# State sums of two of four tiles by accumulating transpositions, in a perceiver layer with a selective scan

## The chip, the cores and the metric

One core of a Trainium2 chip. The metric is the device time in microseconds of one execution, as the median of three runs. Engines: PE (matmul; PEld is its weight load), DVE (vector), ACT (scalar), POOL (GpSimd), and SP, which only issues transfers.

## What is computed

The input is 128 sequences of 32 tokens of 256 features, with 257 context rows for each sequence. All arithmetic is float32 but for the feed-forward weights and activations, which are small integers in bfloat16. Cut to what matters:

```python
x = x + cross_attention(layernorm(x), ctx)
x = x + mixer(layernorm(x))
x = x + feed_forward(layernorm(x))        # quantised weights (-1, 0, 1) and activations (8 bit)

# mixer: 512 channels, 16 states
h = x @ in_w.T + in_b
u = silu(depthwise_conv3(h) + conv_b)
x_dbl = u @ x_proj_w.T + x_proj_b         # 64 columns for delta, 16 for B
delta = softplus(x_dbl[..., :64] @ dt_w.T + dt_b)
state[l, d, n] = exp(delta[l, d] * A[d, n]) * state[l-1, d, n] + delta[l, d] * u[l, d] * B[l, n]
y[l, d] = sum_n state[l, d, n] + u[l, d] * D[d]
out = y @ out_w.T + out_b
```

The change is about the sum over n in the line before the last.

## The kernel before, in words

The 4096 tokens are worked on in 8 blocks of 512 (16 sequences). In the mixer the partitions are 128 of the 512 channels (a tile; there are 4, numbered 0 to 3) and the free dimension is the block's 512 tokens.

A tile has 16 states. They are taken in 11 slots (`SCAN`, line 149): slots 0, 2, 4, 6, 8 hold two states, slots 1, 3, 5, 7, 9, 10 hold one. Each slot goes through the engines so: ACT makes the decay with one exp for each state, from delta, into PSUM (line 641; the buffer of a slot is free when the scan two slots back is done); POOL multiplies w = delta * u with the broadcast B rows into one of 8 state buffers (line 576); DVE runs the scan in place over the state buffer (line 853); and PE adds the states up in the PSUM tensor `acc`, by a matmul of each state with the identity (line 977 is the helper `mm`, which records every plain matmul). A float32 matmul shows as two records. To spare PE work, POOL first adds the two states of slots 2, 4 and 6 of each tile into one (`PAIRED`, line 584, four slots behind its own product), and PE takes that one sum two slots later. When all states of a tile are in `acc`, DVE adds u * D (line 844, the function `y`): for tiles 0 to 2 right after scan 0 of the next tile (`Y_AT`), for tile 3 as the step `y_last`. PE may not start the next tile's sum in `acc` before that.

The order is written out by hand. The program runs in phases of 44 slots, each slot two steps (88 steps). A phase does three things at once: "pre" of block j (attention, conv, silu, x_proj, softplus: table `PRE`), the scan slots of block j-1, and "post" of block j-2 (output projection and feed-forward: table `POST`). The scan slots stand on the odd steps, shifted by `LEAD` for each engine: POOL three slots ahead of DVE, ACT one ahead, PE one behind. The tables give the step at which every engine issues its piece of a part; each engine follows its list strictly in order, and parts on one step follow the order of the tables. The first block's preparation uses `PREPARE` as well; the last block's feed-forward has no scan beside it and uses `LAST`, in which only the order on each engine counts.

Parts the text speaks of. Pre: `stats1`, `rstd1`, `xn1` (first layernorm on DVE, POOL, ACT); `turn1`, `turn2` (transposing the normalised rows on PE); `attn_out`, `x1` (output of the attention, added on DVE); `mix_in` (PE), `u_evac` (ACT), `conv` (DVE, lines 966 and 969), `silu` (ACT, line 740), `x_proj` (PE) and `x_dbl` (ACT), `b_load` (B broadcast to `brep` by DMA), `dt` (PE), `softplus` (ACT, line 764), `times_u` (POOL, line 607). Post: `out_proj`, `x2` (DVE, line 874), `stats3`, `xn3`, `x_max` (DVE, line 882), `x_turn`, `x_evac`; and then eight halves (two to a group of 128 tokens) of `up` (PE, gate and up products), `tanh` (ACT, line 668), `gate` (DVE, line 902), `hidden` (DVE, line 911), and four groups of `h_max` (DVE, line 915), `scale_h` (ACT, line 672), `h_turn` (PE, line 1095, eight 128x128 transpositions), `h_evac` (ACT, line 678), `down` (PE), `finish` (DVE, line 927).

ACT has to load a table when it goes from exp to silu or softplus and when it comes back (rows ACT_TABLE_LOAD).

## Time and profile before

| | |
|---|---|
| median of 3 runs | 1105.43 us (1104.5 to 1112.4) |
| the profiled execution | 1107.78 us, of which the span of the profile is 1106.0 us |
| mean granted PE clock | 0.942 of full speed |
| busy over the span | PE 943.5, DVE 903.5, POOL 857.9, ACT 755.4 us |
| one full phase, 439.1 to 559.5 | 120.4 us |

The profile comes from one execution, so durations and the span belong together; the median is of other executions. PE's matmuls are pipelined and their ends are modelled: the time that a run of matmuls takes of PE is read from the starts, from its own first to the next work's.

### The profile page before, as it was taken

The numbers are of one execution on the slowest core, as the hardware profiler recorded it, in microseconds if no ns is written. First come the engines' busy times: TensorE is split into PE (matmuls) and PEld (weight loads), VectorE is DVE, ScalarE is ACT, GpSimd is POOL, SyncE is SP. The second block draws the span as 40 slices with busy tenths as digits, with TensorE's granted clock in tenths as the row PEclk, the third lists the DMA queues.
The fourth block names the chain that finished last, engine by engine and source line by source line (L and its number), as shares of the span: only waits on it lengthen the run. The fifth ranks groups of instructions, "written<-read, shape, count | busy, mean of one in ns | idle before, by whom it ended". The sixth has DMA issues, their size and how long they took to land.

```text
span 1106.0 us, 12743 instructions
## 1 busy us (share of the span) xinstructions
PE 943.5 (85%) x4007; PEld 491.5 (44%) x4042; DVE 903.5 (82%) x1210; ACT 755.4 (68%) x1320; POOL 857.9 (78%) x617
## 2 busy tenths in 40 slices
PE   6765698899989998999999998999899999777755
PEld 4441344354545453544545454545355454432333
DVE  2312687889998999899998999899989998799935
ACT  1216566787598769877798759876887768655524
POOL 0532999797979988897979797988879797989700
PEclk9778799999999999999999999999999999889967
DMA  9633252414205440525233420544042302200000
GB/s 342 218 131 123 107 178 91 164 60 165 109 21 191 159 166 20 192 77 177 91 120 118 169 111 20 191 153 172 20 172 96 115 20 82 110 0 1 27 12 20
DMA packets 22059, 124.71 MB, mean 113 GB/s; under 512 B 3496, under 2 KB 4136, under 8 KB 9449
## 3 DMA queue, kind: packets, MB, share of 16 engines
q1 hardware_dynamic: 16376, 89.09, 22.1%
q10 hardware_dynamic: 5616, 34.81, 8.2%
q8 instruction: 33, 0.54, 0.2%
q14 instruction: 34, 0.27, 0.1%
HBM read 115.23 MB, written 8.65 MB: 112 GB/s over the span
## 4 chain that ended last, share of the span: by engine, by line
PE 32%; ACT 22%; DVE 21%; POOL 10%; issue 9%; DMA 3%; SPq 1%; ACTq 0%; DVEq 0%; POOLq 0%
PE bank L977 19%; DVE state L853 10%; PE acc L977 10%; ACT decay L641 6%; POOL state L576 5%; DVE sg L902 2%; POOL rstd L539 2%; DVE hid L911 2%; DMA brep<-b_scratch 2%; POOL w L607 2%; ACT u L732 2%; ACT soft L627 2%; DVE hm L915 2%; ACT L740 2%; PE bank L1095 2%
## 5 line engine op out<-in xcount | busy, mean ns | idle before, releaser
L853 DVE TENSOR_TENSOR_SCAN state<-decay,state 128x512 f32<-128x512 f32 (+1 forms) x352 | 589.7, 1696 | 64.7 <-ACT decay L641 48.2
L576 POOL TENSOR_TENSOR state<-w,brep 128x512 f32<-128x512 f32 (+1 forms) x352 | 612.4, 1765 | 24.2 <-PE acc L977 24.0
L977 PE MATMUL acc<-state,ident 128*128 128x512 f32 x832 | 406.6, 608 | 12.9 <-DVE state L853 8.8
L641 ACT ACTIVATE decay<-delta,neg_a 128x496 f32<-128x496 f32 x512 | 327.3, 669 | 75.6 <-DVE state L853 68.9
L977 PEld LDWEIGHTS acc<-state,ident 128*128 128x128 f32 x832 | 148.0, 193 | 166.2 <-issue 110.3
L584 POOL TENSOR_TENSOR state<-state 128x512 f32<-128x512 f32 x96 | 122.2, 1273 | 61.5 <-DVE state L853 61.5
L668 ACT ACTIVATE sg<-bank,ag 128x512 f32<-128x512 f32 x64 | 43.6, 682 | 62.1 <-PE bank L977 61.4
L977 PE MATMUL bank<-xn_t,in_w 128*128 128x512 f32 x128 | 63.6, 632 | 7.6 <-DVE u L969 5.6
L607 POOL TENSOR_TENSOR w<-delta,u 128x512 f32<-128x512 f32 x32 | 39.9, 1266 | 36.2 <-ACT delta L764 36.2
L977 PE MATMUL bank<-out_w,u 128*128 128x256 f32 x256 | 57.4, 382 | 6.7 <-DVE u L844 6.7
L977 PE MATMUL bank<-u,xp_w 128*81 128x512 f32 x64 | 41.1, 803 | 19.2 <-ACT u L740 19.2
L977 PEld LDWEIGHTS bank<-out_w,u 128*128 128x128 f32 x256 | 48.0, 190 | 19.6 <-DVE u L844 13.4
L627 ACT ACTIVATE soft<-x_in,nmr,rstd 128x256 f32<-128x256 f32 x64 | 33.2, 589 | 33.7 <-POOL nmr L542 33.3
L902 DVE SCALAR_TENSOR_TENSOR sg<-sg,bank 128x512 f32<-128x512 f32 x64 | 43.0, 671 | 16.1 <-ACT sg L668 16.1
L678 ACT ACTIVATE hq_t<-bank,unmagic 128x512 bf16<-128x512 f32 x64 | 40.5, 679 | 16.9 <-PE bank L1095 16.8
L1095 PE MATMUL bank<-ident,hid 128*128 128x128 f32 x256 | 37.7, 289 | 12.6 <-ACT hid L672 10.4
L1120 PE MATMUL bank<-ident,soft 128*128 128x128 f32 x128 | 20.6, 312 | 31.7 <-ACT soft L627 31.7
L1095 PEld LDWEIGHTS bank<-ident,hid 128*128 128x128 f32 x256 | 31.0, 148 | 31.9 <-ACT hid L672 16.6
L911 DVE TENSOR_TENSOR hid<-sg,bank 128x512 f32<-128x512 f32 x64 | 42.7, 668 | 0.6 <-PE bank L977 0.2
L977 PE MATMUL bank<-up_q,xq_t 128*128 128x512 bf16 x128 | 40.5, 400 | 3.1 <-DVE hid L911 3.0
L977 PEld LDWEIGHTS bank<-xn_t,in_w 128*128 128x128 f32 x128 | 23.8, 200 | 43.3 <-issue 35.4
L977 PE MATMUL bank<-gate_q,xq_t 128*128 128x512 bf16 x93 | 32.4, 401 | 10.9 <-DVE sg L902 2.8
(137 smaller groups left out, 1306.8 us busy)
## 6 DMA issues: line engine op xcount, KB each, us to landing
keys<-in_keys_t SPq DMA_DIRECT2D x32, 1028.0 KB, 4.8
keys<-in_keys_n SPq DMA_DIRECT2D x32, 1024.0 KB
brep<-b_scratch ACTq DMA_DIRECT2D x32, 1024.0 KB, 6.8
x_scratch<-x_in SPq DMA_DIRECT2D x8, 512.0 KB, 2.6
res<-x_scratch SPq DMA_DIRECT2D x8, 512.0 KB, 3.2
out<-res SPq DMA_DIRECT2D x8, 512.0 KB, 8.6
x_in<-in_x SPq DMA_DIRECT2D x7, 512.0 KB, 5.4
brep<-in_w_gateT SPq DMA_DIRECT2D x1, 1024.0 KB, 13.4
```

The costliest lines, as they stand in the source:

```text
L576: nc.gpsimd.tensor_tensor(state[state_buffer(odd, g)][:, 0:count, :], w[:, m, :].unsqueeze(1).to_broadcast((P, count, TOK)), brep[:, n:n + ...
L584: nc.gpsimd.tensor_tensor(s[:, 0, :], s[:, 0, :], s[:, 1, :], ALU.add).then_inc(paired, 1)
L607: nc.gpsimd.tensor_tensor(w[:, g, :], delta[:, g, :], u[par][:, g, :], ALU.mult)\
L627: nc.scalar.activation(to[:, i, :], x[:, i, :], ACT.Identity, bias=nmr[k][:, i:i + 1], scale=rstd[k][:, i:i + 1]).then_inc(xn_ready[k], 1)
L641: last = nc.scalar.activation(decay[:, to + i, :, 1:LEN], d, ACT.Exp, scale=neg_a[:, m, n + i:n + i + 1])
L668: nc.scalar.activation(sg[g % 2][:, :], bank[:, ffn_banks(g // 2, scan)[0], :], ACT.Tanh, scale=ag[:, g // 2:g // 2 + 1]).then_inc(gate_ta ...
L678: nc.scalar.activation(hq_t[:, k * KT // 2:(k + 1) * KT // 2, :].rearrange("p k t -> p (k t)"), bank[:, ffn_banks(g, scan)[k], :], ACT.Ide ...
L853: nc.vector.tensor_tensor_scan(flat, decay[:, of:of + count, :, :].rearrange("p c q l -> p (c q l)"), flat, 0.0, ALU.mult, ALU.add).then_i ...
L902: nc.vector.scalar_tensor_tensor(sg[g % 2][:, :], sg[g % 2][:, :], 1.0, bank[:, up_a, :], ALU.add, ALU.mult).then_inc(gated, 1)
L911: nc.vector.tensor_tensor(hid[g // 2 % 2][:, half], sg[g % 2][:, :], bank[:, up_b, :], ALU.mult)\
L977: return nc.tensor.matmul(o, l, r, start=first, stop=last)
L1095: last = nc.tensor.transpose(bank[:, to[2 * k // KT], k % (KT // 2) * P:(k % (KT // 2) + 1) * P], hid[g % 2][:, k * P:(k + 1) * P], ident[ ...
```

## The change

Tiles 1 and 2 (`TURNED`) are summed in another way. POOL adds no pairs for them. For each of their 16 states PE issues four 128x128 matmuls with `is_transpose`, the state's 128 tokens as the stationary operand and the identity as the moving one, accumulating in the four quarters of `acc`. So `acc` holds the sum transposed. ACT copies it to a new SBUF tensor `y_t` (behind its exps of slot 2 of the next tile), PE transposes it back into `acc` (in its slot 1 of the next tile, which is DVE's slot 2), and DVE's y comes after scan 2 of the next tile rather than after scan 0. PE's sums of slots 0 to 2 of tiles 2 and 3 are put off to its slot 2. Tiles 0 and 3 are summed as they were, pairs included. All five tables of steps are written anew; of these the diff below shows the entries that the text speaks of.

```diff
--- before.py
+++ after.py
@@ -35,102 +35,102 @@
...
-    ("tanh", [14, 17, 21, 26, 37, 45, 52, 68]),
+    ("tanh", [14, 16, 19, 23, 40, 45, 54, 68]),
-    ("up", [12, 13, 21, 25, 36, 46, 51, 65]),
+    ("up", [12, 13, 17, 22, 40, 47, 51, 67]),
-    ("h_turn", [29, 35, 68, 78]),
+    ("h_turn", [27, 36, 71, 77]),
-    ("h_evac", [32, 36, 71, 77]),
+    ("h_evac", [28, 37, 70, 80]),
...
 PRE = [
-    ("stats1", [1]),
+    ("stats1", [0]),
-    ("xn1", [4]),
+    ("xn1", [6]),
-    ("mix_in", [58, 58, 60, 61]),
+    ("mix_in", [52, 52, 59, 64]),
-    ("silu", [62, 67, 67, 68]),
+    ("silu", [59, 69, 70, 70]),
-    ("x_proj", [67]),
+    ("x_proj", [72]),
-    ("x_dbl", [72]),
+    ("x_dbl", [73]),
-    ("softplus", [81, 87]),
+    ("softplus", [81, 85]),
-    ("times_u", [82, 82, 87, 87]),
+    ("times_u", [81, 82, 83, 85]),
...
 LAST = [
-    ("up", [21, 21, 27, 28, 41, 51, 78, 81]),
+    ("up", [33, 39, 47, 55, 71, 72, 85, 87]),
-    ("tanh", [17, 25, 25, 25, 44, 59, 71, 79]),
+    ("tanh", [25, 31, 47, 56, 58, 78, 86, 86]),
-    ("gate", [16, 27, 32, 38, 70, 72, 78, 79]),
+    ("gate", [25, 38, 42, 66, 72, 80, 84, 85]),
-    ("hidden", [16, 27, 37, 40, 71, 72, 78, 80]),
+    ("hidden", [31, 38, 54, 67, 79, 80, 84, 86]),
-    ("h_max", [33, 52, 76, 86]),
+    ("h_max", [53, 68, 81, 86]),
-    ("scale_h", [26, 29, 77, 81]),
+    ("scale_h", [47, 61, 83, 87]),
-    ("h_turn", [38, 42, 86, 87]),
+    ("h_turn", [61, 74, 84, 87]),
-    ("h_evac", [28, 58, 79, 87]),
+    ("h_evac", [53, 78, 84, 87]),
-    ("down", [40, 73, 86, 87]),
+    ("down", [61, 78, 86, 87]),
-    ("finish", [68, 73, 87, 87]),
+    ("finish", [62, 83, 87, 87]),
...
 PREPARE = [
-    ("total", [12]),
+    ("total", [26]),
-    ("scales", [23]),
+    ("scales", [26]),
-    ("quantise", [44, 50, 52, 59]),
+    ("quantise", [7, 34, 64, 70]),
...
@@ -154,21 +154,34 @@
 
 
 
-PAIRED = (2, 4, 6)
+
+TURNED = (1, 2)
+PAIRED = [m * CPT + c for m in range(TILES) if m not in TURNED for c in (2, 4, 6)]
 PAIR_LAG = 4
-SUMS = [[k for k in range(CPT) if k + 2 * (k in PAIRED) == c] for c in range(CPT)]
-SUM_SLOTS = [c for c in range(CPT) if SUMS[c]]
-
-
-def sums_to(g):
-
-    m, c = divmod(g, CPT)
-    return m * len(SUM_SLOTS) + SUM_SLOTS.index(c + 2 * (c in PAIRED)) + 1
-
-
-def pairs_to(g):
-    m, c = divmod(g, CPT)
-    return m * len(PAIRED) + PAIRED.index(c) + 1
+
+COPY_AT, TURN_AT, READ_AT, SUM_AT = 2, 1, 2, 2
+
+
+def _sums():
+    plan = [[] for _ in range(SLOTS)]
+    for s in range(SLOTS):
+        m, c = divmod(s, CPT)
+        c += 2 * (s in PAIRED)
+        plan[m * CPT + (max(c, SUM_AT) if m - 1 in TURNED else c)].append(s)
+    return plan
+
+
+SUMS = _sums()
+SUM_ORDER = [s for step in SUMS for s in step]
+
+
+def sums_to(s):
+
+    return SUM_ORDER.index(s) + 1
+
+
+def pairs_to(s):
+    return PAIRED.index(s) + 1
 
 
 def slots_to(n):
@@ -270,6 +283,7 @@
         p_t = sb("p_t", [P, 2, P])
         pl_t = sb("pl_t", [P, P])
         z = sb("z", [P, DIM])
+        y_t = sb("y_t", [P, TOK])
         x_dbl = sb("x_dbl", [XROWS, TOK])
 
         xq_t = sb("xq_t", [P, HALVES, TOK], bf16)
@@ -386,8 +400,10 @@
         decay_ready = sem("decay_ready", SLOTS)
         input_ready = sem("input_ready", SLOTS)
         scan_done = sem("scan_done", SLOTS)
-        paired = sem("paired", TILES * len(PAIRED))
-        summed = sem("summed", TILES * len(SUM_SLOTS))
+        paired = sem("paired", len(PAIRED))
+        summed = sem("summed", SLOTS)
+        sums_copied = sem("sums_copied", len(TURNED))
+        sums_turned = sem("sums_turned", len(TURNED))
         y_ready = sem("y_ready", TILES)
 
         mixed = sem("mixed", 2)
@@ -578,7 +594,7 @@
                             w[:, m, :].unsqueeze(1).to_broadcast((P, count, TOK)),
                             brep[:, n:n + count, :], ALU.mult).then_inc(input_ready, 1)
                         done = g - PAIR_LAG
-                        if done >= 0 and done % CPT in PAIRED:
+                        if done in PAIRED:
                             reach(pool, scan_done, b, done + 1)
                             s = state[state_buffer(odd, done)]
                             nc.gpsimd.tensor_tensor(s[:, 0, :], s[:, 0, :], s[:, 1, :], ALU.add).then_inc(paired, 1)
@@ -641,6 +657,10 @@
                             last = nc.scalar.activation(decay[:, to + i, :, 1:LEN], d, ACT.Exp,
                                                         scale=neg_a[:, m, n + i:n + i + 1])
                         last.then_inc(decay_ready, 1)
+                        if m - 1 in TURNED and g % CPT == COPY_AT:
+                            reach(act, summed, b, m * CPT)
+                            reach(act, sums_turned, b, TURNED.index(m - 1))
+                            nc.scalar.activation(y_t[:, :], acc[:, :], ACT.Copy).then_inc(sums_copied, 1)
                     elif part == "mixer_weights":
                         act.wait_ge(w_loaded, 16 * 8)
                         nc.scalar.activation(neg_a[:, :, :], neg_a[:, :, :], ACT.Exp).then_inc(prep_a, 1)
@@ -840,7 +860,10 @@
                         nc.vector.bn_aggr(mv[k][:, i, :], raw[k][:, i, :]).then_inc(moments_ready[k], 1)
 
                 def y(block_, odd, m):
-                    reach(dve, summed, block_, (m + 1) * len(SUM_SLOTS))
+                    if m in TURNED:
+                        reach(dve, sums_turned, block_, TURNED.index(m) + 1)
+                    else:
+                        reach(dve, summed, block_, (m + 1) * CPT)
                     nc.vector.scalar_tensor_tensor(u[odd][:, m, :], u[odd][:, m, :], cols[:, D_SKIP, m:m + 1],
                                                    acc[:, :], ALU.mult, ALU.add).then_inc(y_ready, 1)
 
@@ -852,7 +875,7 @@
                         flat = state[state_buffer(odd, g)][:, 0:count, :].rearrange("p c t -> p (c t)")
                         nc.vector.tensor_tensor_scan(flat, decay[:, of:of + count, :, :].rearrange("p c q l -> p (c q l)"),
                                                      flat, 0.0, ALU.mult, ALU.add).then_inc(scan_done, 1)
-                        if g % CPT == Y_AT and m:
+                        if m and g % CPT == (READ_AT if m - 1 in TURNED else Y_AT):
                             y(b, odd, m - 1)
                     elif part == "qk":
                         qk()
@@ -1003,22 +1026,38 @@
                     after(pe, hid_ready, b, halves)
                     after(pe, hq_t_ready, b, 2 * turned)
 
+                def turn_sums(block_, m):
+                    reach(pe, sums_copied, block_, TURNED.index(m) + 1)
+                    for q in range(GROUPS):
+                        last = nc.tensor.transpose(acc[:, q * P:(q + 1) * P], y_t[:, q * P:(q + 1) * P], ident[:, :])
+                    last.then_inc(sums_turned, 1)
+
                 for part, b, g, odd in slots("tensor", j, par, pre, scan, post):
                     if part == "chunk":
                         m, c = divmod(g, CPT)
-                        if c == 0:
-
-                            reach(pe, y_ready, b, m)
-                        for k in SUMS[c]:
-                            s = m * CPT + k
-                            if k in PAIRED:
+                        if c == TURN_AT and m - 1 in TURNED:
+                            turn_sums(b, m - 1)
+                        for s in SUMS[g]:
+                            n, count = SCAN[s][1:3]
+                            if n == 0:
+
+                                reach(pe, y_ready, b, m)
+                            if s in PAIRED:
                                 reach(pe, paired, b, pairs_to(s))
                             else:
                                 reach(pe, scan_done, b, s + 1)
-                            for i in range(1 if k in PAIRED else SCAN[s][2]):
-                                last = mm(acc[:, :], ident[:, :], state[state_buffer(odd, s)][:, i, :],
-                                          k == 0 and i == 0, k == CPT - 1)
-                        if SUMS[c]:
+                            for i in range(1 if s in PAIRED else count):
+                                one = state[state_buffer(odd, s)][:, i, :]
+                                if m in TURNED:
+
+                                    for q in range(GROUPS):
+                                        part_t = slice(q * P, (q + 1) * P)
+                                        last = nc.tensor.matmul(acc[:, part_t], one[:, part_t], ident[:, :],
+                                                                start=n + i + q == 0,
+                                                                stop=n + i == STATES - 1 and q == GROUPS - 1,
+                                                                is_transpose=True)
+                                else:
+                                    last = mm(acc[:, :], ident[:, :], one, n + i == 0, n + count == STATES)
                             last.then_inc(summed, 1)
                     elif part == "vo":
                         pe.wait_ge(v_loaded, 16 * 4)
```

## Rows read from the trace of the kernel before

**Rows 1.** The page, part 1: busy time, share of the span, instructions.

```profile
PE 943.5 (85%) x4007; PEld 491.5 (44%) x4042; DVE 903.5 (82%) x1210; ACT 755.4 (68%) x1320; POOL 857.9 (78%) x617
```

**Rows 2.** One phase: us; busy PE, PEld, DVE, ACT, POOL; clock, DMA, GB/s.

```profile
439.10:559.50 120.40, 111.53 (x496) 58.24 (x500) 111.05 (x149) 94.03 (x166) 104.89 (x75) 0.99 0.34 123
```

**Rows 3.** Waits of DVE, 318 to 920: us in total, times, longest.

```profile
DVE state L853 <- ACT decay L641: 22.3, 34, 1.7
DVE u L844 <- PE acc L977: 6.1, 5, 1.2
```

**Rows 4.** Waits of ACT and of POOL, 318 to 920.

```profile
ACT sg L668 <- PE bank L977: 38.4, 21, 4.4
...
POOL state L584 <- DVE state L853: 46.0, 25, 2.9
```

**Rows 5.** PE in order of time: start, us, what, count, idle before.

```profile
438.80 5.36 PE L977 MATMUL bank<-u,xp_w 128*81 128x512 f32 x8 [2.19 <-ACT u L740]
443.99 1.04 PE L1095 MATMUL bank<-ident,hid 128*128 128x128 f32 x8
444.86 2.74 PE L977 MATMUL acc<-state,ident 128*128 128x512 f32 x6
447.44 1.04 PE L977 MATMUL bank<-down_q,hq_t 128*128 128x256 bf16 x8
...
559.21 3.66 PE L977 MATMUL bank<-u,xp_w 128*81 128x512 f32 x8 [2.19 <-ACT u L740]
```

**Rows 6.** Groups by form, whole span: busy us, mean ns, idle before.

```profile
L977 PE MATMUL acc<-state,ident 128*128 128x512 f32 x832 | 406.6, 608 | 12.9 <-DVE state L853 8.8 <-DVE u L844 4.1
L641 ACT ACTIVATE decay<-delta,neg_a 128x496 f32<-128x496 f32 x512 | 327.3, 669 | 75.6 <-DVE state L853 68.9 <-issue 5.8
L977 PEld LDWEIGHTS acc<-state,ident 128*128 128x128 f32 x832 | 148.0, 193 | 166.2 <-issue 110.3 <-DVE state L853 42.6 <-DVE u L844 5.7
L584 POOL TENSOR_TENSOR state<-state 128x512 f32<-128x512 f32 x96 | 122.2, 1273 | 61.5 <-DVE state L853 61.5
...
L689 ACT ACTIVATE xn_t<-bank 128x512 f32<-128x512 f32 x32 | 17.6, 588 | 5.1 <-PE bank L1120 5.1
```

**Rows 7.** DVE in order of time, one phase's waits: start, us, idle before.

```profile
441.36 3.41 DVE L853 TENSOR_TENSOR_SCAN state<-decay,state 128x1024 f32<-128x1024 f32 x2 [0.46 <-ACT decay L641]
...
447.71 2.29 DVE L853 TENSOR_TENSOR_SCAN state<-decay,state 128x1024 f32<-128x1024 f32 x1 [1.22 <-ACT decay L641]
...
459.42 2.34 DVE L853 TENSOR_TENSOR_SCAN state<-decay,state 128x512 f32<-128x512 f32 x2 [1.72 <-ACT decay L641]
462.98 0.75 DVE L844 SCALAR_TENSOR_TENSOR u<-u,cols,acc 128x512 f32<-128x512 f32 x1 [1.22 <-PE acc L977]
...
523.07 2.29 DVE L853 TENSOR_TENSOR_SCAN state<-decay,state 128x1024 f32<-128x1024 f32 x1 [0.66 <-ACT decay L641]
...
532.71 0.69 DVE L960 TENSOR_TENSOR x_in<-bank,x_in 128x512 f32<-128x512 f32 x1 [0.41 <-PE bank L977]
```

**Rows 8.** DVE in order of time, the first scans.

```profile
108.90 2.29 DVE L853 TENSOR_TENSOR_SCAN state<-decay,state 128x1024 f32<-128x1024 f32 x1 [16.17 <-POOL state L576]
...
127.67 3.48 DVE L853 TENSOR_TENSOR_SCAN state<-decay,state 128x512 f32<-128x512 f32 x2 [3.03 <-ACT decay L641]
```

**Rows 9.** DVE in order of time, the last feed-forward.

```profile
1083.39 0.48 DVE L927 SCALAR_TENSOR_TENSOR res<-bank,beta,res 128x256 f32<-128x256 f32 x1 [0.33 <-PE bank L977]
1085.30 0.69 DVE L902 SCALAR_TENSOR_TENSOR sg<-sg,bank 128x512 f32<-128x512 f32 x1 [1.42 <-ACT sg L668]
...
1090.87 0.68 DVE L902 SCALAR_TENSOR_TENSOR sg<-sg,bank 128x512 f32<-128x512 f32 x1
...
1094.84 1.22 DVE L915 TENSOR_REDUCE hm<-hid 128x1 f32<-128x1024 f32 x1
...
1102.44 0.48 DVE L927 SCALAR_TENSOR_TENSOR res<-bank,beta,res 128x256 f32<-128x256 f32 x1 [5.10 <-PE bank L977]
```

**Rows 10.** Granted PE clock where x_proj runs: start:end us, busy, clock.

```profile
439.00:441.50 2.50, 2.50 (x4) 0.54 0.00 0
```

118 lines of the change are left out of this document (59 added, 59 removed).

## The prediction, made blind

> **What bounds the kernel now.** I read the busy times first: over the whole run PE is busy 85%, DVE 82%, POOL 78% and ACT 68% of the span [rows 1]. No engine is full on average, but the run has a start and an end in which only part of the work exists, so the next view is the one by stretches. One full phase (44 slots; scan of one block, attention of the next, feed-forward of the one before) takes 120.40 us from 439.1 to 559.5. In it DVE is busy 111.05 us, PE 111.53, POOL 104.89 and ACT 94.03, with a granted PE clock of 0.99 [rows 2]. So DVE and PE are level at 92%. They differ in kind: DVE is in order and its scans are the recurrence that everything else feeds; PE runs ahead or behind within eight state buffers.
>
> What keeps DVE from 111 us is its own waits. In the five full phases (318 to 920) the longest is that of the scan for ACT's decay, 22.3 us in 34 times, or 4.5 us a phase; then y for PE's sums, 6.1 us, once a phase [rows 3]. The scan waits on POOL in no row there: POOL's pair adds wait for DVE instead, 46.0 us, and ACT's tanh waits for PE 38.4 us [rows 4]. POOL therefore has slack, and PE acts on DVE only by way of ACT: a late PE holds tanh, an evacuation or x_dbl, the next exp comes late, and a scan waits. DVE's 9.35 us of idle time in the phase is then the most that a change which leaves DVE's own work alone can win there.
>
> **The change, part by part.** All durations are those of the profiled execution (1107.78 us, span 1106.0), which is 2.35 us above the median of 1105.43.
>
> *PE, sums of tiles 1 and 2.* A plain state sum is two records of a 128x512 matmul against ident; six start at 444.86 and what follows starts at 447.44, so 0.43 us each and 0.86 us a state [rows 5]. With the pairs folded a tile has 13 such sums: 11.2 us. The new form is four 128x128 transpositions a state. Eight transpositions of the same kind start at 443.99 and the next work at 444.86: 0.109 us each, their weight loads hidden [rows 5]. A tile has 16 states, 64 transpositions, 7.0 us, and 0.44 us to turn the sum back. PE so loses 3.8 us a tile, 7.5 us a phase, 60 us in 16 tiles. From both sides: if every transposition in this place cost the whole mean load time of the acc loads, it would be 64 x 0.193 [rows 6] = 12.4 us a tile, 1.6 us more than now with the turn; I take 0.109, the row of the same instruction. None of the 7.5 us is path by itself, because PE is not what DVE waits for, except through ACT.
>
> *POOL, pair adds.* 96 adds of 1273 ns become 48 [rows 6]: 61 us less busy, 7.6 us a phase, and half of their waits. The scans wait for nothing of POOL's, so the direct gain is nothing.
>
> *ACT, one copy for each turned tile.* A PSUM copy of 128x512 takes 588 ns [rows 6], 9.4 us in 16. ACT is idle 26 us a phase [rows 2]; cost nothing if the copy does not wait. What is queued behind it is the exp of slot 3 and all that follows, and the scan waits for that.
>
> *The chain scan, sum, copy, turn, y.* Let T be the end of a turned tile's last scan. The copy stands behind the exp of slot 2 of the next tile, which needs scan 0 (a double scan, 2.29 us [rows 7]) and takes 2 x 0.67 us [rows 6]: T+3.6. The copy ends at T+4.2, four transpositions and the handing over at about T+5. DVE comes to y after scans 0, 1 and 2: T+2.3+1.2+2.3 = T+5.8 at the least. So y is covered by 0.8 us, if PE reaches the last sum and the turn in time. Behind PE's wait stand the deferred sums of slots 0 to 2, the attention work, and ACT for the results of that. Bounds: from -0.1 us a place (the few waits of y at tiles 1 and 2 go) to +1.2 us, the longest wait of y now [rows 3]; over 16 places -2 to +19 us. I take 0, the chain's own count. The eight-buffer ring covers the deferral: POOL is three slots ahead and needs slot 0's buffer again at its slot 8.
>
> *The new plan of steps.* Every table is rewritten, so each wait in the phase may move. Some stay by construction. One is 1.72 us before the scan at 459.42: after a double scan, ACT must do a table load, two softplus, a load and the exp before it. Softplus stays at step 81 and scan 42 behind it. Another is y_last for PE, 1.22 us at 462.98 [rows 7]: tile 3 is summed as before. The second softplus moves from step 87 to 85, ahead of the exp of the next block's slot 0, and stats1 from step 1 to 0, ahead of its scan. That is an exchange: about 3.8 us of ACT now lies before that exp, and 1.9 us of stats lie over it. The waits that PE's queue makes may go. At 447.71 the scan waits 1.22 us; ACT was behind because h_turn of group 2 was queued behind x_proj. In the new plan h_turn (71) is ahead of x_proj (72), but x_dbl follows at 73 rather than 72 and may wait itself. With 0.46 us at 441.36, 0.66 at 523.07 and 0.41 at 532.71 [rows 7], and two of 0.17 and 0.27 us like them, 3.2 us a phase are within reach of a lighter PE. Bounds 0 and -3.2; I take half, -1.6, because the late silu, x_proj and softplus chain is still one chain. Over seven phases with scans (the first and the last are like the five in this): -11.2 us.
>
> *Start.* In the first block softplus of both pairs now runs before the first exp. That saves ACT two table loads, but the first scan (108.90) may come up to 1.6 us later. After it, scans wait for decay 3.03 us at 127.67 [rows 8] and about as much twice before. stats1 and xn1 are also moved. Bounds +1.6 and -5; I take -2. The quantise steps (now 7, 34, 64, 70) come in POOL's order still before the first brep load, and the scales two attention groups later, with nobody waiting: 0.
>
> *End.* The last feed-forward is serial, so its order is its time. Before, tanh and gate of half 3 ran before finish of group 0 (1083.39), half 4 started gate at 1085.30, half 6 at 1090.87, the last h_max at 1094.84 and the last finish at 1102.44 [rows 9]. In the new LAST table finish 0 (62) stands before gate 3 (66), so gate 3, hidden 3 and h_max 1 (0.7+0.7+1.8 us) come after 1083.9 and gate 4 starts at about 1087.1, 1.8 us later. tanh 6 (86) stands behind h_evac 2 (84), which needs h_max 2, scale_h 2 and h_turn 2: gate 6 at 1096.1 rather than 1090.9. up 7 stands behind down 2. The last h_max starts at about 1099.4, 4.6 us later, and 7.6 us from there to the last finish stay. Bounds +3 and +6; I take +4.6.
>
> **Sum.** -11.2 (phases) - 2.0 (start) + 4.6 (end) = -8.6: 1107.8 - 8.6 = 1099.2 as profiled, and 2.35 less as a median, 1096.8. Forecast 1097 us, 0.8% faster. About 1% is what a measurement of this kernel can tell from no change.
>
> **Rivals.** *A, the slack reaches DVE in full.* All of the 3.2 us a phase go, and the replan saves another 1.2 of the waits I held fixed: 7 x 4.4 = 31 us; with -3 and +4.6, 1107.8 - 29 = 1079 profiled, 1076. With the 3.2 alone it is 1084. For it: PE and POOL both get 7.5 us of room. Against: the largest of the waits (1.72 us) stands at a table load that stays.
>
> *B, the PE clock falls where state sums are gone; this one ends slower.* From 439.0 to 441.5 the granted clock is 0.54, the lower of the two levels (1.2 and 2.4 GHz) for nearly all of it [rows 10], after PE had waited 2.19 us for u. The eight x_proj matmuls then took 5.36 us; in the next phase, after the same 2.19 us but with the clock kept, 3.66 [rows 5]. That is 1.7 us of PE and it ended in the 1.22 us DVE wait. Today the sum matmuls fill such gaps. In the second half of tile 2 (steps 53 to 67) the other PE work is little more than mix_in, so transpositions and idle time would be alone there. With two more such falls a phase, each passed on as 1.22 us of DVE, 2.44 x 7 = +17 us, and the 1.6 us gain a phase is not made: 1107.8 + 17 - 2 + 4.6 = 1127 profiled, 1125. One such fall more a phase gives 1116. It decides from 1.3 more falls a phase, where they eat the gain. Against: in 559.2 to 562.9 the clock survived a thin stretch.
> The Trainium skill, "TensorE: Matmul & The Clock Gate", Part 4 (PE-mode transpose), speaks for it: transposing does not count as PE-busy in the same way and does not bring the full clock. No row here has a long run of transpositions alone, so the trace cannot say; by that rule the sum would be rival B's.
>
> *C, the new waits bind.* y, copy and turn miss their 0.8 us of cover by the upper bound in half of the places: +9.6 us, which with the forecast's other terms is 1106: no change. It needs PE's queue to be over 0.8 us late at the turn.
>
> **How the numbers follow.** Forecast 0.50 (1087 to 1105, so 0.20 of it faster by over 1%, 0.30 same). A 0.20, all faster. B 0.18, of it 0.16 slower. C 0.12, of it 0.05 same and 0.07 slower (where every place misses). That makes faster 0.40, same 0.37, slower 0.23. The range 1077 to 1119 leaves out the far end of A and the worse half of B.
>
> **What would show it.** Right: a phase near 118.8 us with DVE still busy 111; PE busy near 104 and POOL near 97 in it; 1024 transpositions in acc for state sums plus 64 turning back, at 0.109 us each when queued; y of tiles 1 and 2 with under 0.3 us of wait; the last gate-to-finish stretch 4 to 5 us longer. Wrong: granted clock under 0.97 in the stretches of tile 2; scans waiting on ACT for over 6 us a phase; y or the copy among the largest waits; or a phase near 116, which would be A.

## The result, and the profile after

The kernel after the change takes 1119.68 us (median of 10 runs) against 1104.80 us for the kernel before on the same chip: ratio 1.0135, 95% interval 1.0105 to 1.0166. The change makes it 1.3% slower; the forecast was 0.8% faster. The profiled execution took 1120.12 us with a span of 1118.3, against 1107.78 and 1106.0 before: 12.3 us to explain (the medians are 14.9 apart).

The page of the kernel after, part 1 (answers to [rows 1]):

```profile
PE 914.5 (82%) x4714; PEld 550.3 (49%) x4714; DVE 902.9 (81%) x1210; ACT 764.5 (68%) x1334; POOL 798.7 (71%) x569
```

PE is 29 us less busy, POOL 59 us less, ACT 9 us more, and DVE unchanged to 0.6 us: the work moved as forecast. The time is therefore DVE's idle time. Phases are read best from y_last to y_last (L844 before, L867 after, the last of a block's four). Before, these starts are 120.25, 120.27, 119.10, 120.21, 121.72, 120.25 and 105.33 us apart; after, 119.87, 122.92, 122.71, 122.96, 119.46, 122.82 and 107.68. The first of them comes at 216.88 rather than 222.46 (start: -5.6), the last finish 59.50 us after the last of them rather than 52.85 (end: +6.65). The seven phases hold the rest, +11.3. (Each is read from one execution; how far the start scatters is said in its place.)

Two phases of the kernel after, a long and a short one (columns as in [rows 2]):

```profile
459.67:582.38 122.71, 107.66 (x584) 65.85 (x584) 110.93 (x148) 95.41 (x168) 97.48 (x69) 0.96 0.33 121
705.34:824.80 119.46, 106.51 (x584) 65.17 (x584) 110.81 (x149) 95.44 (x168) 97.68 (x69) 0.97 0.33 120
```

DVE's work is the same 110.9 us in both, and in [rows 2]. So a full phase of this kernel has two lengths, 119.5 to 119.9 and 122.7 to 123.0, and neither is the forecast's 118.8. The question is what makes it long. Waits of DVE over the five phases from 318 to 920 (as in [rows 3]), then of POOL (as in [rows 4]):

```profile
DVE state L876 <- ACT decay L657: 19.0, 16, 3.0
DVE res L897 <- DMA res<-x_scratch: 7.6, 3, 2.9
DVE u L867 <- PE acc L1000: 6.8, 5, 1.4
```

```profile
POOL ve L552 <- DVE mv L860: 64.3, 10, 9.8
POOL state L592 <- PE acc L1055: 25.8, 10, 3.3
```

The scans wait less for decay in total than in [rows 3] (19.0 for 22.3) and half as often, but the longest is 3.0 us rather than 1.7; a row is new, x2 waiting for the DMA that brings res. y has the same five waits as before, all for tile 3 (releaser L1000): none for a turned tile. POOL waits a lot and nobody for it.

Where x2 waits, in DVE's order of time, early in two of the long phases; the short phase from 705.34 has no such row:

```profile
467.71 0.69 DVE L897 TENSOR_TENSOR res<-bank,res 128x512 f32<-128x512 f32 x1 [2.28 <-PE bank L1000]
...
590.02 0.69 DVE L897 TENSOR_TENSOR res<-bank,res 128x512 f32<-128x512 f32 x1 [1.87 <-DMA res<-x_scratch]
```

The first is put down to PE, whose bank had long been there; the load issued at 460.51 lands 7.1 us later, when the wait ends. With it there are five in the run, 13.0 us, one in each long phase and one in the last. The issues of transfers before the first of the two, of the kernel after and then of the kernel before:

```profile
453.37 0.33 ACTq L774 DMA_DIRECT2D brep<-b_scratch  x1
454.05 0.34 SPq L528 DMA_DIRECT2D out<-res  x1
458.01 0.33 ACTq L774 DMA_DIRECT2D brep<-b_scratch  x1
458.59 0.33 ACTq L774 DMA_DIRECT2D brep<-b_scratch  x1
460.51 0.32 SPq L506 DMA_DIRECT2D res<-x_scratch  x1
```

```profile
455.48 0.33 ACTq L754 DMA_DIRECT2D brep<-b_scratch  x1
456.38 0.33 ACTq L754 DMA_DIRECT2D brep<-b_scratch  x1
457.73 0.34 SPq L512 DMA_DIRECT2D out<-res  x1
466.28 0.32 SPq L490 DMA_DIRECT2D res<-x_scratch  x1
```

The phase itself ends at 459.67 in the first and at 462.98 in the second. Counted from there, the new plan issues the last two brep loads (1 MB each) 5.8 and 5.5 us later and the res load 2.5 us earlier, one on the other. The res load goes in both kernels as soon as the out store ahead of it has landed; that took 6.4 us here and 8.5 before, where it was the store that stood beside the brep loads. The page's part on DMA issues, after (3.2 us to landing before):

```profile
res<-x_scratch SPq DMA_DIRECT2D x8, 512.0 KB, 6.9
```

Why has the phase from 705.34 no such wait? Its issues:

```profile
698.76 0.34 SPq L528 DMA_DIRECT2D out<-res  x1
699.23 0.33 ACTq L774 DMA_DIRECT2D brep<-b_scratch  x1
701.73 0.32 SPq L506 DMA_DIRECT2D res<-x_scratch  x1
```

The x_proj before it was slow (below), so the second brep load comes behind the out store and not 0.7 us ahead of it; the store lands in 2.9 us, and the res load goes 3.6 us ahead of y_last. In this plan a slow x_proj at the end of one phase spares the next one its wait for res; so it does twice more in the kernel with `LAST` put back.

The second kind of wait is at the end of a phase. The end of the phase 582 to 705, DVE in order of time; in the others one row of 1.91 us stands in place of the first two:

```profile
696.07 2.29 DVE L876 TENSOR_TENSOR_SCAN state<-decay,state 128x1024 f32<-128x1024 f32 x1 [1.07 <-ACT decay L657]
701.78 2.34 DVE L876 TENSOR_TENSOR_SCAN state<-decay,state 128x512 f32<-128x512 f32 x2 [3.04 <-ACT decay L657]
705.34 0.75 DVE L867 SCALAR_TENSOR_TENSOR u<-u,cols,acc 128x512 f32<-128x512 f32 x1 [1.22 <-PE acc L1000]
```

PE in that place, then in the short phase after it:

```profile
679.00 0.95 PE L1032 MATMUL acc<-ident,y_t 128*128 128x128 f32 x4 [2.48 <-ACT y_t L663]
679.74 1.92 PE L1134 MATMUL bank<-ident,hid 128*128 128x128 f32 x8
682.66 1.86 PE L1000 MATMUL bank<-down_q,hq_t 128*128 128x256 bf16 x8 [1.00 <-ACT hq_t L698]
...
800.27 0.66 PE L1032 MATMUL acc<-ident,y_t 128*128 128x128 f32 x4 [2.63 <-ACT y_t L663]
800.77 1.04 PE L1134 MATMUL bank<-ident,hid 128*128 128x128 f32 x8
803.57 1.03 PE L1000 MATMUL bank<-down_q,hq_t 128*128 128x256 bf16 x8 [1.76 <-ACT hq_t L698]
```

PE now stands 2.5 us for the copy of the turned sum before it comes to h_turn, down and x_proj. In the first case the clock then falls: eight transpositions take 1.92 us and not 1.04, the down 1.86 and not 1.03. In the second, after the same stop, it holds. Of the six x_proj in full phases this one alone is slow here (4.46 us, the others 3.63). In the kernel before five of six were slow; the sixth, the fast one of [rows 5] at 559.21, ends the one phase of 119.10 us.

The end, DVE (answers to [rows 9]):

```profile
1107.14 1.22 DVE L938 TENSOR_REDUCE hm<-hid 128x1 f32<-128x1024 f32 x1
...
1114.80 0.48 DVE L950 SCALAR_TENSOR_TENSOR res<-bank,beta,res 128x256 f32<-128x256 f32 x1 [5.43 <-PE bank L1000]
```

### The profile page after: what moved, and what is told of

Its sections match the earlier page's. It is cut to its first block, busy times and chain, and to the rows that moved or that the text cites. A ratio compares the mean times of both kernels' runs of the same rounds, so it can differ in the third digit from the quotient of the medians.

```text
span 1118.3 us, 14102 instructions
## 1 busy us (share of the span) xinstructions
PE 914.5 (82%) x4714; PEld 550.3 (49%) x4714; DVE 902.9 (81%) x1210; ACT 764.5 (68%) x1334; POOL 798.7 (71%) x569
## 4 chain that ended last, share of the span: by engine, by line
PE 30%; DVE 27%; ACT 17%; issue 11%; DMA 8%; POOL 6%; SPq 1%; DVEq 0%; ACTq 0%; POOLq 0%
PE bank L1000 18%; DVE state L876 14%; ACT decay L657 5%; PE acc L1000 4%; POOL state L592 4%; DMA res<-x_scratch 3%; DMA out<-res 3%; PE acc L1055 3%; DVE sg L925 2%; DVE raw L856 2%; PE bank L1134 2%; ACT soft L643 2%; DVE hm L938 2%; ACT u L752 1%; DMA brep<-in_w_gateT 1%
## 5 line engine op out<-in xcount | busy, mean ns | idle before, releaser
L1000 PE MATMUL acc<-state,ident 128*128 128x512 f32 x416 | 203.6, 611 | 11.0 <-DVE state L876 10.9
L1055 PE MATMUL acc<-ident,state 128*128 128x128 f32 x1024 | 137.2, 281 | 12.9 <-DVE state L876 8.9
L1055 PEld LDWEIGHTS acc<-ident,state 128*128 128x128 f32 x1024 | 118.9, 145 | 38.2 <-DVE state L876 18.2
L1000 PEld LDWEIGHTS acc<-state,ident 128*128 128x128 f32 x416 | 77.7, 195 | 91.4 <-issue 62.7
L552 POOL TENSOR_TENSOR ve<-mv,eps 128x4 f32<-128x4 f32 x24 | 4.8, 202 | 118.5 <-DVE mv L860 118.5
L1000 PE MATMUL bank<-xn_t,in_w 128*128 128x512 f32 x128 | 74.5, 725 | 7.1 <-ACT xn_t L709 6.0
L600 POOL TENSOR_TENSOR state<-state 128x512 f32<-128x512 f32 x48 | 61.0, 1270 | 21.7 <-DVE state L876 21.7
L1000 PE MATMUL bank<-out_w,u 128*128 128x256 f32 x256 | 57.4, 382 | 6.7 <-DVE u L867 6.7
L1000 PEld LDWEIGHTS bank<-out_w,u 128*128 128x128 f32 x256 | 48.0, 190 | 19.6 <-DVE u L867 13.4
L1000 PE MATMUL bank<-down_q,hq_t 128*128 128x256 bf16 x256 | 37.4, 295 | 14.4 <-ACT hq_t L698 14.2
L692 ACT ACTIVATE hid<-hid,magic,sh 128x1024 f32<-128x1024 f32 x32 | 39.5, 1234 | 12.3 <-DVE sh L944 12.0
L1000 PEld LDWEIGHTS bank<-xn_t,in_w 128*128 128x128 f32 x128 | 28.3, 238 | 39.6 <-issue 30.6
```

The costliest lines, as they stand in the source:

```text
L600: nc.gpsimd.tensor_tensor(s[:, 0, :], s[:, 0, :], s[:, 1, :], ALU.add).then_inc(paired, 1)
L1000: return nc.tensor.matmul(o, l, r, start=first, stop=last)
L1055: last = nc.tensor.matmul(acc[:, part_t], one[:, part_t], ident[:, :], start=n + i + q == 0, stop=n + i == STATES - 1 and q == GROUPS - 1, ...
```

## The experiments

All ratios are to the kernel before, run on the same chip, with their 95% intervals. Theory: the loss is in the plan (the late res, the last feed-forward) and in the clock at x_proj, not in the turned sums.

**Parts of the plan put back, one at a time.** x2 alone:

```diff
-    ("x2", [3, 5]),
+    ("x2", [5, 5]),
```

> The changed kernel with one entry undone: x2 at steps 5, 5 as before instead of 3, 5. Transfer theory (five of the seven phases with scans are about 122.8 us, instead of 119.7 in the two others, because DVE stands at x2 on step 3 for 1.9 to 3.2 us until the res load has landed behind the brep loads): scan 2 now goes ahead of x2 and covers 2.3 us of that, so the waits for the load are under 1 us, the phases near 120.4, and the time 8 to 12 us under the changed kernel's 1119.7, so 1108 to 1112. Clock theory (the phases are long because the PE clock falls twice in each, at h_turn/x_turn and in the second half of tile 2): nothing moves, 1117 to 1123.

Measured 1116.61 us, ratio 1.0115 (1.0081 to 1.0149): above the 1108 to 1112 of the transfer theory, and not clear of the 1.0135 of the kernel after. Yet no x2 waits for a DMA any more in a full phase. Three of its six full phases are still long, 122.5 to 122.6, and just these have a slow x_proj (4.7 us; the others 3.6).

b_load alone, the issue of the brep loads:

```diff
-    ("b_load", [78, 84, 86, 87]),
+    ("b_load", [78, 78, 81, 84]),
```

> The changed kernel with one entry undone: b_load at steps 78, 78, 81, 84 as before instead of 78, 84, 86, 87. Transfer theory, in its sharper form (it is the four 1 MB brep loads issued late that slow the out store and the res load from about 3 us to 7): out and res land early, x2 on step 3 waits for nothing, every phase is near 119.7, the time 1105 to 1109. If x2 is simply too early whatever the loads do, the wait stays and the time is 1116 to 1122. Clock theory: 1117 to 1123.

Measured 1110.09 us, 1.0053 (1.0014 to 1.0091): one wait for res of over a microsecond is left, 1.45 us, and the medians to landing are 3.3 us for res and 8.5 for out, as before the change. Four of the six full phases are short, 119.4 to 119.9; of the two long ones one has a slow x_proj (4.67 us), the other a 2.5 us wait of DVE for tanh instead. This one line holds more than half of the loss.

The order of the last feed-forward alone (table `LAST` of before):

> The changed kernel with the table LAST as before (order of the last feed-forward). Order theory: from y_last to the last finish 59.5 us fall back to 52.9, the time falls by 6.7 us to about 1113; phases unchanged. If the end is long for the clock or the state before it and not for its order, it falls by under 2 us.

Measured 1115.13 us, 1.0083 (1.0049 to 1.0117). The end is 52.8 us from the last y, as before, for 59.5: the order of LAST costs 6.7 us in the profile (5.7 by the ratios, whose intervals overlap a little).

Both of the last two together, the base of what follows ("the mended kernel"):

> The changed kernel with two entries of the plan undone: b_load at 78, 78, 81, 84 and the table LAST as before. The two losses are in different stretches, so they should add: 9.6 us (b_load alone) and 4.6 (LAST alone) under 1119.7, so 1105.5, between 1102 and 1109; the rest over the best phase (two or three of seven phases at 122.6 for a clock fall at x_proj) stays.

Measured 1106.37 us, 1.0016 (0.9979 to 1.0053): no difference from before can be measured. This is the turned sums together with the rest of the new plan, and it is a balance: in the profiled execution the first y_last comes at 215.27 for 222.46, and the seven phases take 834.4 us for 827.1, four of the six full ones with a slow x_proj (4.75 to 4.84 us).

**Plan and sums apart.** The new sums with the tables of before, then the kernel before with the tables of after (there are four, `POST`, `PRE`, `LAST` and `PREPARE`, not the five that the section on the change speaks of):

> The turned sums of tiles 1 and 2 alone: all four tables POST, PRE, LAST, PREPARE as before the change. Plan theory (transposed sums themselves are worth a little, the new tables lose it): phases 118.5 to 120.5, no wait of x2 for the res load, start and end as before the change, 1098 to 1106. Clock theory: the clock falls twice a phase here too, phases 121 to 123, 1112 to 1122. Rival: the new copy and turn were placed for the new plan and bind in the old one: y of tiles 1 and 2 or the copy wait over 1 us each, 1108 to 1125.

> The kernel before (plain sums, pair adds on all tiles) with the four tables POST, PRE, LAST and PREPARE of the changed kernel. If the plan alone loses the time: x2 waits for the res load, the last feed-forward is 59.5 us long, 1112 to 1122. If the plan and the turned sums only belong together (plan good for a PE that is 7 us lighter): PE is behind, scans wait more for ACT, over 1120. If the loss is the turned sums' (clock falls, waits for the copy): 1100 to 1110, because the start is 5.6 us shorter and the end 6.7 longer, with one clock fall a phase.

Measured 1145.98 us, 1.0358 (1.0302 to 1.0413), and 1199.51 us, 1.0840 (1.0771 to 1.0908). Waits of DVE in the first of them:

```profile
DVE u L867 <- PE acc L1032: 40.7, 15, 3.6
```

The first is slower than any of its expectations. With the old plan y of the turned tiles waits for the turn, 2.7 us each; with the new one never. So it is the new plan that gives the turn its cover. Each half alone is far worse than both together.

**What holds the clock.** To the kernel before are added, after the last out_proj, 72 transpositions of ident into a free bank; in the second kernel instead 9 plain float32 matmuls of 512 columns (18 records):

```diff
+for i in range(72):
+    nc.tensor.transpose(bank[:, E, i % 4 * P:(i % 4 + 1) * P], ident[:, :], ident[:, :])
```

> A probe of the clock in the kernel before: after the last out_proj, where PE otherwise waits about 8 us with the clock falling from 1.00 to 0.50, it does 72 more float32 transpositions of ident into an idle bank (7.8 us at 0.109 each; extra work whose result is not used). If transpositions hold the clock like matmuls: granted clock 1.00 until they end, each 0.109 us apart, x_turn and the first up at the full rate too, and the end 1 to 3 us shorter. If they do not: the clock falls to 0.50 within them as it does now, the later ones come 0.21 to 0.22 us apart and x_turn is up to 5 us late.

> The same probe with 9 plain float32 matmuls of 128x512 (18 records, 7.7 us at 0.43 each; extra work whose result is not used) in place of the 72 transpositions. Both theories: granted clock 1.00 until they end, x_turn at 0.109 us a transposition, end 1 to 3 us shorter than in the kernel before.

PE of the first, and its stretches (clock next to last but two); then a stretch of the kernel before at the same place in its work, and one of the second kernel:

```profile
1054.45 8.02 PE L1052 MATMUL bank<-ident 128*128 128x128 f32 x72
```

```profile
1054.00:1064.00 10.00, 8.47 (x75) 8.12 (x73) 4.81 (x18) 3.25 (x7) 1.52 (x4) 1.00 0.01 2
1064.00:1074.00 10.00, 4.81 (x22) 1.90 (x22) 4.83 (x9) 4.92 (x8) 0.00 (x0) 1.00 0.00 0
```

```profile
1067.00:1077.00 10.00, 7.05 (x19) 3.00 (x20) 3.05 (x5) 4.29 (x7) 0.00 (x0) 0.50 0.00 0
```

```profile
1060.00:1068.00 8.00, 3.95 (x14) 2.08 (x14) 1.95 (x10) 4.13 (x7) 0.00 (x0) 0.63 0.00 0
```

Transpositions hold the clock: 1.00 through them and for 10 us behind, where the kernel before has 0.50. The matmuls held it no longer than the transpositions did. The 10 us behind are not sure: four more profiles below have the same 72 transpositions (this kernel again, and three others). All four show 1.00 through them, but in two of the others the clock fell 4 us behind their end. The stretch from the last y to the last finish is 50.0 us with the first and 51.0 with the second, for 52.85 (one execution each, 1101.97 and 1100.68 us). The first kernel timed:

> The kernel before with the 72 transpositions after its last out_proj, timed: the one look gave 1101.97 us with 50.0 us after the last y, against 52.85. Theory: the held clock gives back 2 to 3 us, 1101.5 to 1102.8 against 1104.5, ratio 0.9975. Rival (the look's gain was the scatter of single runs): 1104 to 1105.

Measured 1104.17 us for 1106.41, 0.9975 (0.9947 to 1.0003). It has the lowest ratio of those timed, and its gain is at the limit of what these runs can tell: the interval reaches 1. The end is 50.0 us again.

**Is the lighter PE to blame for the clock?** The mended kernel with `is_transpose=False` in the turned sums, so that the same 64 instructions a tile run as float32 matmuls (two records each, twice PE's time):

> The changed kernel with b_load and LAST undone and the sums of tiles 1 and 2 as plain float32 matmuls of the same operands (state quarter stationary, ident moving, the same transposed result) in place of is_transpose: twice the PE time, 0.215 us each, so 7 us more a phase, PE busy near 114. Clock theory (a lighter PE is why the clock falls): the falls at mix_in and x_proj go, granted clock 0.98 to 0.99 in the phases as in the kernel before; whether the time falls depends on how much of the 7 us PE hides: 1100 to 1112. Rival (the clock is incidental, the turned form has its price by its waits): the clock stays near 0.96, and with PE slower the time is over 1112.

Measured 1173.27 us, 1.0590 (1.0559 to 1.0620), over 1112 as the rival had it. PE is busy 120.6 us a phase, not 114, every full phase takes 129.5 to 129.9 us, and their granted clock is 0.96, no better than in the kernel after. But x_proj is slow in one of the six full phases alone (4.87 us, the others 3.63), for four of six in the mended kernel, and PE stops for 2.0 us at the turn, not 2.5. Both the load of PE and its stop changed, so this run does not say which of them the clock at x_proj hangs on.

**The place of copy and turn.** In the mended kernel, the copy one slot earlier; then copy, turn, read and sums all one slot earlier; then this with the 72 transpositions at the end:

```diff
-COPY_AT, TURN_AT, READ_AT, SUM_AT = 2, 1, 2, 2
+COPY_AT, TURN_AT, READ_AT, SUM_AT = 1, 1, 2, 2
```

> The changed kernel with b_load and LAST undone (1106.4 so far, phases of 119.9 or 122.4) and the copy of the transposed sum one slot earlier on ACT (COPY_AT 1 instead of 2). Theory of the stalled PE: PE stands 2.5 us at the turn of tile 2 for the copy, which ACT has behind its exps of slot 2, and the clock falls on that idle time, into x_proj, in every second phase or so, 2.7 us each; with the copy a slot (1.3 to 2 us of ACT) earlier the wait is under 1.5 us, the fall at x_proj goes in most phases, which are then 119 to 120, and the time is 1096 to 1102. Rival (the fall there comes of PE having too little work, whatever it waits for): the wait at the turn shrinks but phases of 122.4 stay as frequent, 1104 to 1108.

Measured 1118.88 us, 1.0099 (1.0065 to 1.0132). The theory missed: PE no longer stops at the turn, but 2.29 us before h_turn and 1.90 before down instead, the clock falls at x_proj in every phase, and the six full ones are all long, 122.4 to 122.9. The stop only moved.

> As e9_copy_early, and turn, deferred sums and y one slot earlier too (COPY, TURN, READ, SUM at 1, 0, 1, 1). Stalled-PE theory: the copy is ready 0.7 us after PE comes to the turn, y is 3.5 us behind the last scan and still covered, POOL waits less for state buffers (45.7 us now); 1094 to 1102, at best below e9. If one slot is too little cover: y waits over 1 us for the turn in 14 places, as in the run with the old plan, 1108 to 1125.

> As e10_turn_early with the 72 filling transpositions after the last out_proj. From the single run of the probe (y_last to last finish 50.0 us instead of 52.9) 2.9 us less than e10; by the mean of both expectations 1092 to 1099, which would be below the kernel before by 0.6 to 1.1%.

Measured 1151.29 us, 1.0377 (1.0348 to 1.0407), and 1155.56, 1.0414 (1.0378 to 1.0449). With y one slot earlier PE waits up to 4.7 us for DVE's y before it may begin tile 3, and phases are 127 to 129 us: the cover that the chain has in the code as changed is not to be shortened.

**Is it the clock, or x_proj's end?** These four start from the mended kernel. Fourteen transpositions ahead of the third down, where PE waits 1.8 us:

> The version with b_load and the last block's plan put back (1106.4 us, phases of 119.9 and of 122.5), and beside it 14 transpositions of ident ahead of the third down, in the 1.8 us in which TensorE waits for hq_t there. Theory (the clock that falls at x_proj makes the long phase, and the fall is started by the idle 2.5 us before the turn of y_t, 3 us earlier): the fill comes too late to hold the clock, so long phases stay, 1104 to 1108. Rival 1 (the wait before down starts the fall): x_proj takes 3.6 us in every phase, all phases 119.8 to 120, total 1096 to 1098. Rival 2 (the fill delays down and x_proj): every phase 0.5 to 1 us longer, 1110 to 1114.

Measured 1107.89 us, 1.0012 (0.9982 to 1.0042). The time is the theory's, and long phases stay (122.5, 122.1 and 122.0; the others 119.8 to 120.5), though x_proj takes 3.6 us in every one, as rival 1 had it. So the trace separates the two causes. (The phase of 122.5 has no fall ahead of x_proj, but a wait of 1.64 us for res.) PE in a phase of 122.06 us:

```profile
558.42 1.81 PE L1134 MATMUL bank<-ident,hid 128*128 128x128 f32 x8
560.02 2.63 PE L1143 MATMUL bank<-ident 128*128 128x128 f32 x14
562.49 1.04 PE L1000 MATMUL bank<-down_q,hq_t 128*128 128x256 bf16 x8
563.37 3.60 PE L1000 MATMUL bank<-u,xp_w 128*81 128x512 f32 x8
```

Here the clock fell and came back before x_proj (0.50 from 558.6 to 561.9, 1.00 from 562.0), which ran at full speed, but started 5.44 us after the turn, and the scan then waited 3.04 us. Where the fill took 1.69 us, x_proj started 4.2 us after the turn and the scan waited 1.91 us. So the slow clock does its harm by making x_proj end late, wherever it falls ahead of that end.

The fourth mix_in behind the up projection, to fill the stop before the turn; and the same with both fills:

```diff
-    ("mix_in", [52, 52, 59, 64]),
+    ("mix_in", [52, 52, 59, 67]),
```

> The same version with one due time changed, the fourth mix_in from slot 64 to 67: by the order of the program its 4 matmul records (1.9 us) then stand between the up projection and the turn of y_t, where TensorE now idles 2.5 to 2.6 us. Theory (that idle time starts the fall of the clock at x_proj, and the fall makes a phase of 122.5 us out of one of 119.9): the idle stretch shrinks to 0.8 us, x_proj takes 3.6 us at a granted clock of 1.00 in nearly every phase, the waits for the third tile's y and the conv after it stay away, phases 119.8 to 120.2, total 1096 to 1099. Rival (the long phase has another cause, and the slow x_proj only goes along with it): clock held, phases still 122.5, total 1105 to 1108. Second rival (the fourth conv now waits for its matmul): 0.5 to 1 us more a phase, 1110 and over.

> The late mix_in, the 14 transpositions ahead of the third down, and 72 transpositions of ident after the last out_proj, as in the fill of the kernel before. By the theory the phases are 119.8 to 120 (twice 2.5 us less than those of the late mix_in if a fall is left there) and the end after the last y is 50.0 us and not 52.8: 1093 to 1096. If neither fill adds anything to the late mix_in: 1096 to 1099. If the fills get in the way: over 1100.

Measured 1135.27 us, 1.0241 (1.0203 to 1.0280), and 1118.64 us, 1.0110 (1.0069 to 1.0150). The move missed: ScalarE's evacuation waits for the late mix_in, 2.62 us, and the copy of y_t stands behind it, so PE stopped 3.6 us before the turn instead of 2.6. The pair tells something all the same. PE without and with the fill ahead of down, the same place of a phase:

```profile
566.90 1.11 PE L1032 MATMUL acc<-ident,y_t 128*128 128x128 f32 x4 [3.61 <-ACT y_t L663]
...
570.70 1.86 PE L1000 MATMUL bank<-down_q,hq_t 128*128 128x256 bf16 x8 [0.98 <-ACT hq_t L698]
572.36 5.62 PE L1000 MATMUL bank<-u,xp_w 128*81 128x512 f32 x8
```

```profile
563.13 0.66 PE L1032 MATMUL acc<-ident,y_t 128*128 128x128 f32 x4 [3.61 <-ACT y_t L663]
...
567.69 1.04 PE L1000 MATMUL bank<-down_q,hq_t 128*128 128x256 bf16 x8
568.56 3.60 PE L1000 MATMUL bank<-u,xp_w 128*81 128x512 f32 x8
```

Same plan, same stop of 3.61 us; with the fill x_proj takes 3.60 us and not 5.62. With the fill every x_proj of a full phase takes 3.60 us. The three full phases in the middle of the run go from 126.3 to 122.9 us, 3.4 us each (the first full phase only from 124.8 to 124.0). Without the fill one x_proj of six kept the clock by itself (3.63 us), and its phase was 123.5. That is the price, in this plan, of a fall of the clock that lasts into x_proj, shown by one edit and once more inside one run (the end fill lies outside these phases). The filled kernel still has the stop and a shorter fall, and its scans wait 3.04 us in every phase.

Last, x_proj ahead of the third down, with the end fill:

```diff
-    ("h_evac", [28, 37, 70, 80]),
+    ("h_evac", [28, 37, 71, 80]),
-    ("down", [28, 61, 72, 81]),
+    ("down", [28, 61, 73, 81]),
```

> The version with b_load and the last block's plan put back (1106.4 us), with ScalarE's copies of hq_t of the third half one slot later, behind its three silus, and the third down one slot later, behind x_proj; also the 72 transpositions after the last out_proj. x_proj then waits for the last silu alone and starts about 1.2 us earlier where the clock is held and 2.0 us earlier where it falls. Theory (what makes a phase long is that x_proj ends late, by the fall of the clock or by anything else, since ScalarE's copy to x_dbl, the hidden half and delta queue up behind it): in every phase the last wait of the scans for decay is 1.9 us or less, never 3.0, also where the clock falls at x_proj; phases 119.4 to 120.3; with the end at 50.0 to 51.5 the total is 1093 to 1099, ratio 0.990 to 0.995. Rival (the slow clock costs elsewhere too, or hq_t and down, moved back, bind instead: finish of the third half or the scans' decays wait for them): phases of 121 to 123 remain, total 1102 to 1110.

Measured 1112.47 us, 1.0058 (1.0031 to 1.0085): the rival in its phases, over its range in time. PE in two phases:

```profile
437.15 5.36 PE L1000 MATMUL bank<-u,xp_w 128*81 128x512 f32 x8 [2.48 <-ACT u L760]
...
559.91 3.66 PE L1000 MATMUL bank<-u,xp_w 128*81 128x512 f32 x8 [2.48 <-ACT u L760]
```

x_proj starts 4.0 us after the turn, against 4.2 to 4.3 where the clock held and 5.0 where it fell in the mended kernel. The silu before it waits 0.92 us for DVE's last conv, so copies of hq_t moved out of its way gave little, and PE, which now stands 2.48 us before x_proj, found the clock low there in five of six full phases. The last wait for decay is 2.58 us in every phase, so the theory's 1.9 was missed too. The phases of these two are 122.7 and 121.1 us: a slow x_proj costs 1.7 us here, and it does so by the third down, now behind it: the finish waits 1.67 us in the first phase and not at all in the second.

The end was 50.0 us again, as in the kernel before with this fill. It was not in the other two kernels that have it: with the late mix_in it came out at 53.0 us (54.9 without the fills), and with the turn one slot earlier at 53.0 for 52.1, which is no gain at all.

## Why the prediction was wrong

**The step that failed is "the new plan of steps": -11.2 us for the seven phases, measured +11.3.** The prediction took the waits of before, asked which of them a lighter PE could shorten, and counted half. Those went in part: over the seven phases the scans wait for decay 23.8 us for 29.8, and x_in no longer waits for PE (2.5 before). Others grew in their place, that of the conv for ACT's u above all; after, then before, from the first y_last to the last, columns as in [rows 3]:

```profile
DVE u L989 <- ACT u L756: 7.1, 6, 1.4
```

```profile
DVE u L966 <- ACT u L736: 2.1, 6, 0.3
```

The gate's wait for tanh went from 5.6 to 7.2 us, and res was waited for 13.0 us, before 0.5. Take the 12.5 us away and the phases are about 1 us shorter than before, not 11.2 (an estimate: it takes each wait to be passed on in full). Like against like nothing was won: a phase in which neither new wait occurs is 119.5 to 119.9 us, and the one phase of before with a fast x_proj 119.1 (its scans wait 3.5 us for decay, in the phase ahead of it 4.7). The 120.4 us phase that the forecast started from had one slow x_proj in it. What the step did not do is walk the queues past each edited line. Two things that it never priced made new waits:

- `b_load` later and `x2` earlier. The res load now starts 1.9 and 2.5 us behind the last two brep loads and takes 6.9 us to land for 3.2. Five times it came late, 13.0 us together, enough for the 11.3 by which the phases grew. With x2 put back the waits are gone, with b_load put back 3.6 us of them are left, in five small ones; b_load alone brought the ratio from 1.0135 to 1.0053. Both lines are in the tables that the change rewrites, though not in the part of the diff shown above.
- The stop at the turn. The prediction asked whether y would wait for PE (it did not, in any phase), and not what PE does while ACT brings the copy: it stands for 2.5 us at tile 2's turn, shortly ahead of x_proj, and waits again for hq_t. The clock fell there in one full phase of six in the profile of after, in three with x2 put back, in one with b_load put back, and in four in the mended kernel. ACT then waits for x_dbl, for h_turn's bank and for a second dt, and the scans find their decay 1.07 and 3.04 us late instead of 1.91. The new plan also put x_proj nearer to those who need it: its start is 20 to 21 us ahead of y_last, before it was 23 to 24. So a fall costs about 2.6 us of a phase now (mended kernel: 122.5 for 119.9 in the mean); before it cost 1.1 (119.1 against 120.2), and came in nearly every phase. With x2 put back the waits for res went and two more slow x_proj came; that is why it brought so little.

**Rival B named a real cost, but not the one that made this kernel slow.** It said that the clock falls where state sums are gone, that each fall is passed on as 1.22 us, and that the time is 1116 for one more fall a phase and 1125 for two. 1119.7 lies between, and that is chance. The clock did fall more, 0.92 for 0.942 in the mean. One of the new falls stands where B put it, in the second half of tile 2, in every full phase: at mix_in (granted clock 0.50 from 660 to 665 us, for one), and the conv behind it waits 0.8 to 1.4 us for ACT's u, 0.35 before. But at x_proj the clock was low in one full phase of six, before in five, and the 11.3 us are the waits for res. Only with these mended is a fall at x_proj what makes a phase long, and then it costs 2.6 us, twice B's price. Whether the falls come of PE's lighter load, as B said, or of its stops was not separated: the fuller PE of the matmul form had its x_proj slow in one phase of six and also stopped for less time.

**The rule of the Trainium skill did not hold here.** The Trainium skill says in "TensorE: Matmul & The Clock Gate", Part 4 (PE-mode transpose), that transposing does not count as PE being busy in the same way and that the full clock does not engage for it. Here the 72 float32 transpositions in a row kept it at 1.00. They also brought it back: in the kernel with 14 of them ahead of down it was 0.50 from 558.6 to 561.9, PE did nothing but transpositions in that time, and from 562.0 it was 1.00.

**What held.** PE's loss of work: 1024 transpositions in 137.2 us of busy time, though 107 us a phase rather than 104: the 137.2 us are 8.6 us a tile, and the count had 7.0. POOL 97.5 for 97. DVE 110.9 for 111. ACT 95.4. The cover of the chain scan, sum, copy, turn, y: 0.8 us by the count, no wait for a turned tile in the trace, 2.7 us each as soon as the plan is taken away. So rival C did not come about, nor rival A (whose sum takes the start at -3 where the forecast has -2, 1 us).

**Start and end.** The start was taken at -2.0, with -5 as its bound, and gave -5.6 in the profiles. That miss is not shown: the profile of before and the three of its end fills have the first y_last at 218.5 to 222.5 us (220.3 in the mean); those of after, of its four kernels with x2, b_load or LAST put back and of the one with 14 transpositions ahead of down have it at 214.9 to 219.1 (217.1), so -3.2. Which of the moved parts does that was not tried. The end was taken at +4.6 and cost +6.65, outside its bound of +6: the order of tanh and finish was read rightly, and the last h_max to the last finish is 7.66 us as counted, so the missing 2 us are ahead of it. Putting the table back gave all 6.7 us back in the profile.

The cause of any single fall of the clock stays open. It is not that PE stops for longer: in the profiles of after, of its four kernels with x2, b_load or LAST put back, and of the one with 14 transpositions ahead of down, the stop at the turn was 2.47 to 2.49 us in the 13 full phases in which the clock fell behind it, and 2.62 or 2.63 in the 23 in which it held. Open is also whether a version without the falls would beat the kernel before: a fill during the stop at the turn itself was not tried.

## What to carry to other kernels

When a hand-written order is rewritten, price every line that moved, the transfers first: ask for each one what else is in flight at its new time. Where an engine gains work that comes back from another one, ask not only who waits for the result but what the engine does meanwhile; here a stop of 2.5 us ahead of a long matmul that others wait for was followed in some phases by a fall of the clock that cost as much again. A phase with two lengths is a gift: compare a long with a short one of the same run before building anything.

## What the runs showed of the hardware that was not expected

- Transpositions of float32 hold the granted clock: 72 of 128x128 in 8.02 us at 1.00, in all five profiles that have them. In three it was still 1.00 in the 10 us behind, in which PE was busy 4.8 us (first fill kernel); in the other two it fell 4 us behind them.
- Transpositions alone brought the clock back from 0.50 (558.6 to 561.9) to 1.00 (from 562.0).
- A load of 0.5 MB took 6.6 to 7.8 us to land when issued within 2.8 us of two loads of 1 MB from another queue, and 3.1 to 3.3 us where the last of these had gone 9.8 us or more before it. A store of 0.5 MB ahead of it in its own queue landed in 8.5 us when the last two of these loads had been issued 2.3 and 1.4 us before it, and in 2.9 us in the phase in which the next of them was issued 0.5 us behind it.
